# Neighbour sums of a graph network: one sum in flight instead of four

## The reference

```python
seg_sum = jax.ops.segment_sum(nodes[senders], receivers, num_segments=num_nodes)
counts = jax.ops.segment_sum(jnp.ones_like(receivers, dtype=nodes.dtype), receivers, num_segments=num_nodes)
h_neigh = seg_sum / jnp.maximum(counts, 1.0)[:, None]
h = jnp.concatenate((nodes, h_neigh), axis=1)
out = h @ W_left + b_left
out = out + nodes @ W_right
```

## Time and profile before

| what | value |
| --- | --- |
| time, median of 3 runs | 10952.63 us (10929.3 to 10963.74) |
| the profiled execution, its own time | 10945.58 us |
| its span in the profile | 10944.0 us |
| TensorE busy / POOL busy / VectorE busy | 6721.0 / 5884.4 / 4976.1 us |
| granted TensorE clock, mean over the span | 0.772 |

### The profile page before, as it was taken

One profiled execution on the slowest core, in us unless ns is written; L12 is line 12 of the kernel. 1 busy time (PEld: TensorE's weight loads), 2 busy tenths in 40 slices (PEclk: granted clock), 3 DMA queues, 4 the chain that ended last, 5 costly groups with the idle time before them and its releaser, 6 DMA issues. The chain is left out here.

```text
span 10944.0 us, 123234 instructions
## 1 busy us (share of the span) xinstructions
PE 6721.0 (61%) x26920; PEld 4969.2 (45%) x26921; DVE 4976.1 (45%) x11169; ACT 2223.2 (20%) x4973; POOL 5884.4 (54%) x6163
## 2 busy tenths in 40 slices
PE   8577777777777877757886446544444534434442
PEld 4355555555555765546764334333323423223331
DVE  6576666666666666655554222222222311112124
ACT  4344444444444211111110000000000101001110
POOL 2255555555555116665554677677777655554542
PEclk9788888888888987778888667666666767667775
DMA  3455555655565332225553333333333311111114
GB/s 128 149 169 170 168 173 171 172 169 170 170 173 165 103 110 72 74 69 155 151 153 108 102 105 109 103 95 87 92 92 89 96 26 33 30 28 31 33 33 152
DMA packets 658020, 1226.05 MB, mean 112 GB/s; under 512 B 168236, under 2 KB 410080, under 8 KB 657747
## 3 DMA queue, kind: packets, MB, share of 16 engines
q0 software_dynamic: 296176, 717.44, 24.3%
q1 hardware_dynamic: 334117, 467.16, 13.5%
q10 hardware_dynamic: 27580, 39.79, 1.0%
HBM read 1087.91 MB, written 144.07 MB: 113 GB/s over the span
## 5 line engine op out<-in xcount | busy, mean ns | idle before, releaser
L970 POOL DMA_INDIRECT e_kv<-KV,e_idx x1712 | 1621.6, 947 | 1386.6 <-PE e_psA L1087 787.0
L2558 POOL DMA_INDIRECT s_x<-XN,s_idx x1712 | 1773.1, 1036 | 588.4 <-issue 525.6
L2585 PE MATMUL s_psA<-s_x,s_oh 128*128 128x257 f32 x1712 | 680.2, 486 | 1050.4 <-DVE NS L2627 490.3
L1646 POOL DMA_INDIRECT SD<-o_pay,o_pos x880 | 931.2, 1058 | 642.4 <-DVEq L46 314.0
L2954 POOL DMA_INDIRECT t_g<-G,t_idx x1024 | 972.5, 950 | 315.5 <-issue 313.9
L1071 PE MATMUL e_psQ<-QA,e_oht 128*128 x3424 | 1035.0, 455 | 136.4 <-issue 78.9
L2627 DVE TENSOR_TENSOR NS<-s_psA,NS 128x257 f32 x856 | 364.3, 426 | 1561.8 <-DMA X<-b_xo 913.8
L3136 PE MATMUL t_psY<-t_w,t_H 128*128 128x256 f32 x1600 | 445.4, 446 | 905.4 <-issue 518.5
L2585 PEld LDWEIGHTS s_psA<-s_x,s_oh 128*128 128x128 f32 x1712 | 382.0, 239 | 1233.1 <-issue 1135.0
L1071 PEld LDWEIGHTS e_psQ<-QA,e_oht 128*128 128x128 f32 x3424 | 743.6, 226 | 286.4 <-issue 159.1
L3136 PEld LDWEIGHTS t_psY<-t_w,t_H 128*128 128x128 f32 x1600 | 360.7, 229 | 994.0 <-issue 825.5
(11 more groups left out here) (601 smaller groups left out, 11795.2 us busy)
## 6 DMA issues: line engine op xcount, KB each, us to landing
o_dbf<-DBF SPq DMA_DIRECT2D x128, 512.0 KB
f_w<-in_L_ffn_Wd_dram SPq DMA_DIRECT2D x57, 1024.0 KB
e_relb<-REL SPq DMA_DIRECT2D x107, 512.0 KB
o_dlo<-DLO SPq DMA_DIRECT2D x128, 256.0 KB
e_kv<-KV,e_idx POOLq DMA_INDIRECT x1712
s_x<-XN,s_idx POOLq DMA_INDIRECT x1712
YD<-t_y ACTq DMA_DIRECT2D x50, 512.0 KB
h_yt<-YD SPq DMA_DIRECT2D x10, 2560.0 KB
```

What stands on the lines that cost most here:

```text
L970: pool.indirect_dma_start(kv[:, s, t, :], None, k.KV, bass.IndirectOffsetOnAxis(ap=idx[:, s, t:t + 1], axis=0)).then_inc(kv_in[s][g], 16)
L1646: pool.indirect_dma_start(self.k.SD, bass.IndirectOffsetOnAxis(ap=self.pos[:, s, j:j + 1], axis=0), self.pay[:, s, j, :], None).then_inc(s ...
L2558: pool.indirect_dma_start(x[:, s, t, 0:C], None, k.XN2, bass.IndirectOffsetOnAxis(ap=idx[:, s, t:t + 1], axis=0)).then_inc(x_in[s], 16)
L2585: pe.matmul(psA[:, u % 4, 0:C + 1], oh[:, o, 2 * u, :], x[:, s, 2 * u, :], start=True, stop=False)
```

## The change

TensorE waited, ahead of step u, for VectorE's add of step u - 4, which frees the PSUM buffer that step u writes. Now it waits for the add of step u - 1. So at most one sum is in flight: TensorE computes one, VectorE adds it, and then TensorE computes the next. The four buffers of psA stay as they are, and each engine issues the same instructions in the same order.

```diff
--- before.py
+++ after.py
@@ -2581,7 +2581,7 @@
                 at(pe, oh_done, i, 1, 0)
                 loaded(pe, x_in[s], i, s, per=CT, slots=XS)
                 for u in range(CS):
-                    at(pe, acc_done, i, CS, u - 4)
+                    at(pe, acc_done, i, CS, u - 1)
                     pe.matmul(psA[:, u % 4, 0:C + 1], oh[:, o, 2 * u, :], x[:, s, 2 * u, :], start=True, stop=False)
                     pe.matmul(psA[:, u % 4, 0:C + 1], oh[:, o, 2 * u + 1, :], x[:, s, 2 * u + 1, :], start=False, stop=True)\
                         .then_inc(agg_ps, 1)
```

## The result

The kernel after takes 11257.3 us (median of 4 runs, 11229.42 to 11270.39), the kernel before 10951.31 us beside it (4 runs, 10929.3 to 10963.74): a ratio of 1.028, 95% interval 1.0262 to 1.0298, or 306 us more. The profiled execution took 11270.39 us, its span is 11268.7, against 10944.0.

What follows compares the result with a forecast made beforehand. Gathers on POOL bound nearly all of the neighbour sums; after the change, turns would. Longer chunks +191 us, own products' signal +55, clock lift -15: +231 on 10,945.6, with the median's 7 and loop edges 11,190 us; range 11,000 to 11,450.

Steps and rivals of the forecast that it cites:

- The turn: Neighbour sums: add, hand-over, sum, hand-over now alternate, 2.88 us at the half clock (0.50, 1.2 GHz), 1.87 at the full.
- The chunks: Neighbour sums, eight a chunk: 50 with a node tile at 27.6 us, 57 plain at 23.2, against POOL's 22.2.
- Late signals of single sums: 0: Neighbour sums: no time added for TensorE's signals reaching VectorE late, since one awaited sum's signal came at once.
- The first chunk: Start of the neighbour sums: given no term of its own, counted among the 50 chunks of 27.6 us.
- The own products' signal: Chunks with a node tile: signal to the add of X late by 0 to 2.06 us; middle 1.1 taken, +55 us.
- The lift of the clock: After the own products, an unbroken TensorE run may raise the clock for one or two sums: -15 us.
- B: Rival, faster: no late signals, clock full for most turns, POOL alone sets the pace: 10,833 us; chance 0.07.
- A: Rival: signals late at every turn, 8.8 us each, about 15,900 us; chance 0.14, 0.05 of it for every signal late.
- The milder form: Rival: one signal in twenty to one in ten late by some 5 us, 11,400 to 11,620 us; chance 0.09.
- C: Rival: clock full for a sixth to a third of the turns, 11,067 to 11,001 us; chance 0.10.
- The two rules that were weighed: Skill rules: one, read backwards, said giving up buffers costs nothing, 10,953 us; the other, spacing completion increments, favoured fewer late signals.
- The other signs: Profile after: POOL idle some 50 x 5 + 57 x 1 us at index copies, last add near 8,780, TensorE's waits ended by adds.

Runs made afterwards that it cites:

- Half the gathers: Every second gather left out, both matmuls of a sum reading one group: kernel before 9786.62 us (ratio 0.8903), kernel after 11163.05 us (1.0156).
- the filler: Kernel after with one more matmul, of constants, on TensorE behind each sum, its result unread: 11175.38 us, ratio 1.0227.
- the half sums: Second matmul of each sum left out, in the kernel after (one sum in flight): 9578.01 us, ratio 0.9953, on a chip running the kernel before in 9627.06.
- third group: Runs on the 9627.06 us chip; those cited: kernel after with a spare signal per sum, 9942.04 us, or POOL at most three chunks ahead, 9941.53 us.
- half sums with four in flight: Second matmul of each sum left out, in the kernel before: 9607.5 us, ratio 0.9979.
- two in flight: TensorE waits for the add of step u-2, in place of u-4 in the kernel before: 11004.75 us, ratio 1.0057.

## Why the prediction was right

11,190 us was forecast, 11,000 to 11,450; measured are 11,257, slower as said.

*The turn.* 2.88 us at the half clock was forecast, 2.89 is measured in the loops (2.71 outside of them), and the clock is 0.50 but for one stretch of 7 us in chunk 1. The nearest row by kind (rests between sums, 61% busy) told it rightly against the one at 95% busy. Half the gathers shows that this pace stands alone, the filler that it hangs on the clock, the half sums that it costs only beyond POOL's 22.2 us. The turn of 1.87 us that was worked out for the full clock is 1.95 us in the filler's trace.

*The chunks.* Tile chunks: 27.6 forecast, 27.58 measured. Plain chunks: 23.2 forecast, 24.47 measured, 56 x 1.27 = 71 us more. Without late adds they take 23.33 (third group): 7 of the 71. The other 64 are the step "Late signals of single sums: 0", which was mis-sized: 61 us of late adds lie in these chunks.

*The first chunk* was counted as one of 50 at 27.6 us; it takes 85.1, +57.5 us, all of it late signals of TensorE: 26 us of them on adds 3 to 6, 14 on ScalarE's copy, 12 on the add of X and 6 on the next chunk's first add. The prediction had put the long idle times of VectorE down as gone. The kernel before loses them too, but its pair catches up behind it, as POOL is then four chunks ahead: its next three chunks take 13.3, 9.8 and 16.9 us, those of the kernel after 25.0, 24.6 and 26.3.

*The own products' signal*, +55 us, fell: in chunks 1 to 49 the add of X comes 0.3 us or less behind the product. In the new order the prompt case is the rule. In the old one both occurred about as often: in 26 of its 50 chunks the add of X comes over 0.6 us late, as in the earlier trace rows, and by up to 13.0 us. *The lift of the clock*, -15 us, fell as well: it came once, in chunk 1, where the own products and the two sums behind them ran at the full clock. B's "each time" did not hold of the kernel before either: its bias product took 0.69 us in 28 chunks and 1.22, the half clock, in 22.

The sum: 2,739 us forecast from first to last add; +57.5 + 71 - 55 + 15 gives 2,827, measured are 2,826. Against 2,508 before that is +318, where I had +231. The median grew by 306. That the forecast came within 67 us of it is in part luck: two losses that it did not have, 128 us, stand against 40 us net of two terms that did not come, and the first chunk's loss is more than half of the 87 us by which the stage was missed.

*Two losses that cancel.* From first to last add the old order takes 2,508 us. Its bare pace, free of late signals, has no trace; I estimate it at 2,388, from the 2,368 of half sums with four in flight and the 20 us by which the kernel before is slower than that kernel on the third chip. So it loses 120 us. The new one takes 2,826, 122 above its own bare pace of 2,704 (third group). So as far as this estimate goes the bad first chunk and the late signals cost both orders about the same here, though the old one has ten times the late adds: where gathers run four chunks ahead, most of a late add is caught up; where turns set the pace, each one counts. What is left is the difference of the two bare paces, some 316 us; the times on the chip without such losses differ by 315.

*The rivals.* A (late signals at every turn) is excluded. The milder form came by its count, 50 late adds in 856, one in seventeen, but at 2 us each: 102 us, of which 40 lie in the first chunk, where the old order has them too. B was right that late signals become fewer and wrong that this brings anything, as the clock is not full. The filler is B with its missing half added, and it too fell short, with 582 us of late adds. C's lift of the clock occurred once.

*The two rules that were weighed.* The Trainium skill, "TensorE: Matmul & The Clock Gate", section "HAM oscillation — how this bites in real kernels", read as saying that giving the buffers up costs nothing, does not hold here: +306 us. So read it does hold for the half sums, 0.9953. The page itself says less: that adding the second buffer brought nothing in one kernel, after its loop had been reordered. The Trainium skill's rule in "VectorE: DVE Perf Modes", section on the TRN2 errata, is to space increments that several engines raise densely on completion. It is given there against a deadlock; that it bears on late signals was the prediction's reading. The change spaces them and late adds fell from 1,111 to 102 us; but two in flight spaces them too, in part, and left 1,016, and where signals were doubled there was nothing late. No run here confirms the rule.

*The other signs.* POOL stands idle for 374 us at the copies in the loops where 307 were forecast, the last add is at 8,859 in place of 8,780, and of the 879 us that TensorE waited ahead of line 2585 the profile puts 609 down to the adds and 40 to gathers; both of the first two carry the late signals.

*What stays open*: what makes a signal late, and what the loops add to a turn. Lateness is not a matter of the number of sums in flight alone (two against four, and the first chunk, the same in both orders), it is rarer in turns at the half clock and frequent in turns with the filler, rarer with half of the gathers, and absent on one chip with the same instructions. Of the in-chunk sums of the kernel after that ended while POOL gathered, none of 169 was late in the first 10 us of an unbroken row of gathers, one of some 200 up to 16 us, 14 of some 200 up to 25 us, and five of the few beyond. Some 13 more were late that had ended while POOL rested, up to 2.5 us behind its last gather. That is a correlation, which the third chip does not share.

## What to carry to other kernels

Before giving up buffers between two engines, add up one turn, producer, hand-over, consumer, hand-over, at the clock that TensorE will have with those rests, and hold it against the pace of whatever feeds them: 2.89 us a turn lost 3% here, 2.04 lost nothing. Take the turn from the part of the code where most of them run: between 2.71 and 2.89 us lies the border for the plain chunks of this kernel. An engine that is mostly idle in a stage is no sign of slack, since the old order needed its slack to catch up after a bad first chunk and late signals. Read the first chunk of a stage by itself before multiplying a chunk by its count, and measure a change on more than one chip where the trace shows waits that no instruction explains.

## What the runs showed of the hardware

- In both orders signals of TensorE can arrive late while POOL issues gathers, or just behind them: 276 adds in the kernel before, by 4 us in the mean (1,111 us) and by up to 10.8 us. In the first chunk the adds are 10 to 11 us apart in both. ScalarE's signal from TensorE is 14.4 us late there in the kernel after. On one chip of those used here, whose gathers took as long, there was none, and the same kernel took 9,627 us in place of 10,951.
- In a steady turn of sum and add TensorE is busy for 36 of 53 us, all at 0.50; one more matmul in each turn (two passes, 0.44 us each in the mean) lifted the granted clock to 0.83.
- A turn is 2.89 us inside the loops and 2.71 in the chunks written out beside them, at the same instructions on TensorE and VectorE: add to sum 0.14 and 0.05 us, sum to add 0.27 and 0.15. Gathers beside it make no difference: of the 643 turns 61 had none, and of the 68 shorter ones 38 had some.
